# Attention on one core: value products in four 32-wide column tiles, denominators from pair sums

## The reference

```python
q, k = x @ wq_s, x @ wk_s                  # 8 heads of 16, over x normalised
attn = softmax(q @ k.T * 16 ** -0.5)       # per image and head, 1024 x 1024
v = x @ wv_r                               # 2 x 16 columns, shared by all heads
per_head = attn @ v                        # 1024 x (2 x 16), for each of 8 heads
sim = softmax over the 2 retrievals of (u . per_head) * 16 ** -0.5
out = sum over the 2 retrievals of sim * per_head
x = x + out @ w_out
```

## Time and profile before

| | us |
|---|---|
| median of 3 executions | 5733.49 |
| lowest, highest | 5732.6, 5741.53 |
| span of the profiled execution | 5736.7 |
| PE busy | 4699.7 (82%) |
| DVE busy | 3076.5 (54%) |
| ACT busy | 1975.9 (34%) |
| POOL busy | 633.7 (11%) |
| mean granted PE clock | 0.898 |

### The profile page before, as it was taken

One profiled execution on the slowest core, in us unless ns is written; L12 is line 12 of the kernel. 1 busy time (PEld: TensorE's weight loads), 2 busy tenths in 40 slices (PEclk: granted clock), 3 DMA queues, 4 the chain that ended last, 5 costly groups with the idle time before them and its releaser, 6 DMA issues. The chain is left out here.

```text
span 5736.7 us, 63937 instructions
## 1 busy us (share of the span) xinstructions
PE 4699.7 (82%) x19695; PEld 1764.3 (31%) x19695; DVE 3076.5 (54%) x5438; ACT 1975.9 (34%) x2773; POOL 633.7 (11%) x882
## 2 busy tenths in 40 slices
PE   4599999947699898888888888896699999855423
PEld 2233333315122222222222222223344444443212
DVE  4777777748666666556555555553300000357663
ACT  3211111127044444444444444455343434412200
POOL 1000000007101111111110110014100000201201
PEclk9799999979599999999999999998899999966655
DMA  1344444427411112222122222201000000112404
GB/s 63 79 103 91 92 99 92 95 82 262 66 21 19 19 21 27 27 27 27 23 27 27 27 27 27 27 5 50 29 0 0 0 0 0 54 64 80 122 0 128
DMA packets 173099, 290.74 MB, mean 51 GB/s; under 512 B 23207, under 2 KB 98989, under 8 KB 171453
## 3 DMA queue, kind: packets, MB, share of 16 engines
q1 hardware_dynamic: 144696, 252.65, 20.8%
q10 hardware_dynamic: 23808, 25.17, 1.2%
q0 software_dynamic: 4368, 10.07, 0.6%
HBM read 92.39 MB, written 67.63 MB: 28 GB/s over the span
## 5 line engine op out<-in xcount | busy, mean ns | idle before, releaser
L1474 DVE TENSOR_REDUCE at_mx<-at_side 128x1 f32<-128x512 f32 x2048 | 1336.6, 687 | 452.2 <-PE at_side L1387 445.8
L1543 ACT ACTIVATE at_P<-at_S 128x1024 f32<-128x1024 f32 x1024 | 997.1, 1024 | 1345.6 <-PE at_S L1412 1281.0
L1422 PE MATMUL at_pv<-at_P,at_rvb 128*64 128x512 f32 x4096 | 1113.1, 627 | 71.6 <-issue 54.1
L1387 PE MATMUL at_side<-at_ko,at_qo 96*128 96x512 bf16 x2048 | 757.7, 400 | 63.2 <-DMA at_ko<-qk 38.0
L1412 PE MATMUL at_S<-at_qo,at_ko 99*128 99x512 bf16 x2048 | 594.9, 381 | 22.6 <-DMA at_qo<-at_mrow 22.3
L1784 PE MATMUL ff_ph<-ffn_Y,ff_w 128*128 (+1 forms) x1024 | 525.5, 595 | 9.3 <-DMA ff_b<-in_b_dram 9.3
L1814 ACT ACTIVATE ff_hs<-ff_ph,ff_b 128x512 f32<-128x512 f32 x512 | 351.7, 687 | 525.3 <-PE ff_ph L1784 525.3
L1798 PE MATMUL ff_po<-ff_hs,ff_w2s 128*128 128x512 f32 x1024 | 523.2, 593 | 0.0
L616 PE MATMUL la_acc<-la_rep,la_wagg 128*32 128x512 f32 x4096 | 511.2, 606 | 1.1 <-DMA la_rep<-la_pad 1.1
L773 DVE SCALAR_TENSOR_TENSOR la_dwq<-la_pad,la_taps,la_dwq 128x1024 f32<-128x1024 f32 x384 | 491.7, 1280 | 7.2
L1833 DVE SCALAR_TENSOR_TENSOR X<-ff_po,ffn_b2w,X 128x512 f32 (+1 forms) x32 | 24.0, 751 | 823.8 <-PE ff_po L1798 823.8
(11 more groups left out here) (410 smaller groups left out, 4194.6 us busy)
## 6 DMA issues: line engine op xcount, KB each, us to landing
la_rep<-la_pad SPq DMA_DIRECT2D x512, 162.2 KB, 3.6
qk<-ap_part SPq DMA_DIRECT2D x32, 768.0 KB, 3.7
at_qo<-qk SPq DMA_DIRECT2D x96, 256.0 KB, 9.8
at_ko<-qk SPq DMA_DIRECT2D x96, 256.0 KB, 20.1
n_ln_xs<-X SPq DMA_DIRECT2D x96, 256.0 KB, 2.3
X<-in_x_dram SPq DMA_DIRECT2D x4, 2048.0 KB, 22.2
proj<-la_y POOLq DMA_DIRECT2D x32, 256.0 KB, 2.3
lan_y<-proj SPq DMA_DIRECT2D x8, 1024.0 KB, 5.0
```

Source lines behind the costliest of these rows:

```text
L1387: return pe.matmul(side[bank][:, :], qo[1 - u][0:KQ, s, i * C:(i + 1) * C], ko[1 - u][0:KQ, s, h * CH:(h + 1) * CH], start=True, stop=True)
L1422: last = pe.matmul(pv_acc[hp][64 * i:64 * i + 64, :], rvb[u][:, j, :], P[k % 2][:, 2 * hp + i, :], start=(j == 0), stop=(j == 7))
L1474: v.reduce_max(mx[:, n // 2, n % 2:n % 2 + 1], side[bank][:, :], AX.X).then_inc(side_saved, 1)
L1543: a.activation(P[k % 2][:, 2 * hp:2 * hp + 2, :], S[hp][:, :, :], ACT.Exp).then_inc(p_ready, 1)
```

## The change

Values of four heads go as four 32-wide column tiles into one accumulator `num`, with the 32 values alone as weights. For the denominators POOL adds the exponentials of two steps into one (`pair`), and PE multiplies the sum by 32 columns of ones, four heads side by side, into `den` (`totals`), after the values of each even step. `P` has four buffers in place of two; `exps` of an even step waits for the denominators that read its buffer. The order in a group becomes half first, then quad, so that half of the queries is finished for all heads in mid-slot, and retrieval, tokens, back and output run in two halves. Maxima run four a step in all 32 steps. The loads, maxima rows and `ub` are split in halves; values go through `u` in memory (columns 128 to 159 of it) in place of the tile `RV`.

```diff
-                        v.tensor_copy(us[w][:, 2 * h:2 * h + 2, :], puv[h][:, :, 0:C])
-                        v.tensor_copy(RV[:, bass.ds(4 * n + 2 * h, 2), :], puv[h][:, :, C:C + RVW]).then_inc(uv_saved, 1)
+                        v.tensor_copy(us[w][:, 2 * h:2 * h + 2, :], puv[h][:, :, :]).then_inc(uv_saved, 1)
...
-FIRST_MAX = 3
-LAST_MAX = STEPS - 4
-PER_STEP = -(-MAX_UNITS // (LAST_MAX + 1 - FIRST_MAX))
-EXP_AT, SUM_AT, OUT_AT, WOUT_AT = 13, 15, 19, 22
+QUAD = 4
+TOKENS_AT = (2, 18)
+BACK_AT = (5, 22)
+WOUT_AT = (6, 23)
+EXP_AT = (28, 12)
+SUM_AT = (30, 14)
+ROWS_AT = (17, 1)
...
-        P = [m.sb(f"P{u}", [C, 4, CH]) for u in range(2)]
+        P = [m.sb(f"P{u}", [C, QUAD, CH]) for u in range(4)]
...
+                    if not last and not is_first(b):
+                        sp.wait_ge(s_ready, 64 * b)
+                        load(b + 1, 1 - u, 1)
+                    if not last:
+                        wait_if(sp, pv_done, 32 * b)
+                        values_of(b + 1, 1 - u)
...
-                        sp.wait_ge(s_ready, 64 * b + 64)
-                        load(b + 2, u)
+                        sp.wait_ge(s_ready, 64 * b + 48)
+                        load(b + 2, u, 0)
...
+                def pair(b, i):
+                    g.wait_ge(p_ready, 64 * b + 4 * i + 4)
+                    g.wait_ge(pv_done, 32 * b + 2 * i + 1)
+                    a = 2 * i % 4
+                    g.tensor_tensor(P[a][:, :, :], P[a][:, :, :], P[a + 1][:, :, :], ALU.add).then_inc(pair_done, 1)
...
+                def slot(b, u, last):
+                    post = not is_first(b)
+                    for i in range(16):
+                        pair(b, i)
+                        if i == 0 and post:
+                            retrieve(b - 1, 0, 6, None)
+                        if 2 <= i <= 8 and post:
+                            retrieve(b - 1, 1, i - 2, side_at(b, ("tokens", 1, 3), last))
+                        if i >= 10:
+                            retrieve(b, 0, i - 10, side_at(b, ("tokens", 0, 3), last))
...
-                    for i in range(2):
-                        last = pe.matmul(pv_acc[hp][64 * i:64 * i + 64, :], rvb[u][:, j, :], P[k % 2][:, 2 * hp + i, :],
+                    pe.wait_ge(p_ready, 64 * b + 2 * k + 2)
+                    for i in range(QUAD):
+                        last = pe.matmul(num[32 * i:32 * i + 32, :], rvt[u][:, j, :], P[k % 4][:, i, :],
                                          start=(j == 0), stop=(j == 7))
...
+                def totals(b, k):
+                    j = (k - 2) % 8
+                    if j == 0:
+                        wait_if(pe, den_saved, 4 * b + k // 8)
+                    pe.wait_ge(pair_done, 16 * b + k // 2)
+                    for i in range(QUAD):
+                        last = pe.matmul(den[32 * i:32 * i + 32, :], K["ones"][:, 0:32], P[(k - 2) % 4][:, i, :],
+                                         start=(j == 0), stop=(j == 6))
+                    last.then_inc(den_done, 1)
...
+                        for part in range(3):
+                            for w in work[(part * len(work) + 1) // 3:((part + 1) * len(work) + 1) // 3]:
+                                fill(w, b, u, side_base(b) + at, bank_of(b, at)).then_inc(side_ready, 1)
+                                at += 1
+                            if part < 2:
+                                if k + 2 < STEPS:
+                                    scores(b, u, k + 2, part)
+                                elif not last:
+                                    scores(b + 1, 1 - u, k + 2 - STEPS, part)
+                        values(b, u, k)
+                        if k % 2 == 0 and not (first and k == 0):
+                            totals(b, k)
...
                 def exps(b, k):
+                    if k % 2 == 0:
+                        wait_if(a, den_done, 16 * b + k // 2 - 1)
                     for hp in range(2):
                         a.wait_ge(s_ready, 64 * b + 2 * k + hp + 1)
-                        wait_if(a, pv_done, 32 * b + k - 1)
-                        a.activation(P[k % 2][:, 2 * hp:2 * hp + 2, :], S[hp][:, :, :], ACT.Exp).then_inc(p_ready, 1)
+                        a.activation(P[k % 4][:, 2 * hp:2 * hp + 2, :], S[hp][:, :, :], ACT.Exp).then_inc(p_ready, 1)
...
+                        if k % 8 < 2 and (k >= 8 or not first):
+                            if k >= 8:
+                                save(b, k // 8 - 1, k % 8)
+                            else:
+                                save(b - 1, 3, k % 8)
```

More of the change, by code:

```diff
@@ L1210, with side_work @@
 MAX_UNITS = 128
-VW = 2 * RH * DH
-FIRST_MAX = 3
-LAST_MAX = STEPS - 4
-PER_STEP = -(-MAX_UNITS // (LAST_MAX + 1 - FIRST_MAX))
-EXP_AT, SUM_AT, OUT_AT, WOUT_AT = 13, 15, 19, 22
-def side_work(k, post, following):
+QUAD = 4
[5 more added lines that the diff above has]
+ROWS_AT = (17, 1)
+def side_work(k, first, last):
+    post = not first
     work = []
     if post:
[L1222 to L1231, removed]
+        if k == ROWS_AT[1]:
+            work.append(("rows", 1))
+        for n in range(4):
+            if k == TOKENS_AT[0] + n:
+                work.append(("tokens", 1, n))
+        for h in range(2):
+            if k == BACK_AT[h]:
+                work.append(("back", h))
+            if k == WOUT_AT[h]:
+                work.append(("wout", h))
+    for n in range(4):
+        if k == TOKENS_AT[1] + n:
+            work.append(("tokens", 0, n))
+    if not last:
+        if k == ROWS_AT[0]:
             work.append(("rows", 0))
+        work += [("max", n) for n in range(QUAD * k, QUAD * k + QUAD)]
     return work
+TAIL = ([("tokens", 1, n) for n in range(4)] + [("back", 0), ("wout", 0), ("back", 1), ("wout", 1)])
 def phase_attn(nc, K, D, X):
-    SIDE1 = MAX_UNITS + 1
-    SIDE2 = SIDE1 + 12
+    SIDE0 = MAX_UNITS + 2
+    SIDE1 = sum(len(side_work(k, True, False)) for k in range(STEPS))
+    SIDE2 = sum(len(side_work(k, False, False)) for k in range(STEPS))
+    SIDE3 = sum(len(side_work(k, False, True)) for k in range(STEPS))
+    assert SIDE2 % 2 == 0
     with Mem(nc, "at") as m:
@@ L1316, in slot @@
+                for z in range(2):
+                    load(0, 0, z)
+                values_of(0, 0)
+                for z in range(2):
+                    load(1, 1, z)
+                for z in range(2):
+                    rows(0, 0, z)
                 def slot(b, u, last):
-                    if not isinstance(b, int) or b:
-                        sp.wait_ge(side_ready, side_at(b, OUT_AT, ("back", 1), following=not last))
-                    sp.dma_start(ub[:, :, :], D["u"][:, bass.ds(8 * b, 8), :]).then_inc(u_in, 16)
+                    if not last and not is_first(b):
+                        sp.wait_ge(s_ready, 64 * b)
+                        load(b + 1, 1 - u, 1)
@@ L1375, in _ @@
+                over(g, B, slot)
+                retrieve(B - 1, 0, 6, None)
+                for part in range(7):
+                    retrieve(B - 1, 1, part, TAIL_BASE + 4)
             @block.tensor
@@ L1440, in slot @@
+                for z in range(2):
+                    pe.wait_ge(op_in[0][z], 192)
+                    for n in range(64 * z, 64 * z + 64):
+                        fill(("max", n), -1, 1, n + z, (n + z) % 2).then_inc(side_ready, 1)
+                    fill(("rows", z), z - 1, 1, 64 + 65 * z, (64 + 65 * z) % 2).then_inc(side_ready, 1)
                 def slot(b, u, last):
-                    post = not isinstance(b, int) or b > 0
+                    first = is_first(b)
                     at = 0
-                    pe.wait_ge(rv_ready, b + 1)
@@ L1571, in slot @@
                             exps(b + 1, 0)
-                        if k == EXP_AT and post:
-                            softmax2(b - 1)
-                        if k % 8 == 7:
-                            save(b, k // 8, post, last)
+                        if k == EXP_AT[1] and not first:
+                            softmax2(2 * b - 1)
+                        if k == EXP_AT[0]:
+                            softmax2(2 * b)
                 over(a, B, slot)
-                softmax2(B - 1)
+                for what in range(2):
+                    save(B - 1, 3, what)
+                softmax2(2 * B - 1)
 def phase_norm(nc, K, X, Y, tag, tokens=None):
@@ L2451, in build @@
         phase_linatt_norm(nc, K, D, X)
[L2452 to L2455 removed]
+        phase_attn_prep(nc, K, D, X)
+        phase_attn(nc, K, D, X)
         with Mem(nc, "ffn") as m:
```

359 lines of the change are left out of this document (191 added, 168 removed).

## The result

The changed kernel takes 5851.4 us (median of 4 runs, 5838.26 to 5856.9) against 5733.92 in the same comparison: 1.020 times as long, interval 1.0185 to 1.0214. I had forecast 5649, a gain. The profiled execution spans 5852.8.

A forecast was written before the change was run, and what follows sets the result against it. PE, 91% busy in attention, sets the pace now; after the change a ring of exponentials and denominators binds. Terms -193 + 60 - 19 - 9 + 56 + 8 + 13 = -84 gave 5649 us, range 5575 to 5755.

The forecast's parts named there:

- 14 x 142.9 + 60: Middle slots: 142.9 us each without load waits, against 138.9, plus 60 for waits and low clock at five loop jumps.
- First slot: Attention's first slot, without retrieval and with one copy pair less: 136.3 us against 127.8, +8.
- last: Attention's last slot, without maxima: 110.5 us against 98.0, +13.
- -19: Prologue: half the loads land 13 to 14 us sooner and the 4.91 wait for maxima rows goes; -19 us.
- tail: After attention, only the second half of the last image's retrieval is left, with POOL operations halved; -9 us.
- The ring: Attention steps: even-step exponentials wait for denominators, next scores for them; 8.06 us per two steps against 8.36.
- I take 0, by the nearest row that runs: DVE's splitting of maxima rows during POOL's pair sums, twice a slot: taken to cost 0, from a 0.284 us row.
- The upper end, +69: Row splitting waits for the rest of the pair sum: 2.3 us, 2 x 15 times, +69.
- The clock: Rival: PE's clock falls for a tenth of each slot, +150, giving 5800; chance 0.06.
- Loads: Half loads remove the waits at slot starts, -193 with clock; +60 returns at the loop jumps.
- POOL: POOL's pair sums in attention: 4.5 us each, 16 a slot, hidden with 6.8 of 9.2 us used.
- the second: Rival: DVE's row splitting waits for POOL's pair sums, +69, giving 5718; chance 0.25.

The follow-up runs named there:

- e1: The changed kernel with the remainder of the row maxima (`mleft`) in the free half of the PSUM side buffer instead of SBUF; 5739.2 us.
- after: The changed kernel itself, as measured and profiled, against the kernel before; 5851.4 us.
- e5: e1 with ACT's two copies of a group's sums behind the exponentials of the same step instead of ahead; 5567.6 us.
- e4: The kernel before with only its loads divided into halves of four heads, asked for at different steps; 5553.1 us.
- e7: e5 plus a separate buffer for POOL's pair sums and the second half-load asked for at step 2 of its own slot; 5359.9 us.
- e8: e4 with the second half-load asked for at step 2 of its own slot instead of step 30 of the one before; 5532.2 us.

## Why the prediction was wrong

The miss is 202 us: -84 forecast, +117.5 measured. In the profiled execution it is made of these, with about 1 left over:

- *Slots 1 to 14*, 159.85 on average, in sum 2238 against 14 x 142.9 + 60 = 2061: +177.
- First slot 142.3 against 136.3, last 121.1 against 110.5: +17.
- First value product at 1559.3 where -19 meant 1555, tail 27.5 us where -9 from 34 meant 25: +7.

The slots 1 to 14 of e1 (1701.4 to 3822.9) divide the 177. Undisturbed steps, 14 x 145.2 against 14 x 142.9, are 32 of it. The jumps and the slow steps of e1 are 89 where I had 60, which is 29. What after takes more than e1, 2238 against 2121, is the row splitting, 117.

Point by point:

- **The ring was right.** Pitches of 5.08 and 3.14 (5.00 in the peeled slots) against 4.91 and 3.15: 8.22 against 8.06. A slot from e1's undisturbed steps is 145.2, not 142.9: +32 over 14 slots. Blocks of 1.01, the 0.21 to the exponentials, and saves of 4.70 and 5.49, 2.0 more than plain steps (1.9 a group in the sum), came as read.
- **The step that failed: "I take 0, by the nearest row that runs".** The row was read at a time when POOL stood still, so it could not bear on an overlap. (The reduction at 2217.62, which the prediction puts beside POOL, doesn't overlap it either: POOL's last operation there ended at 2216.78. Others, as that at 2208.74, did, at their usual pace, but they read PSUM.) The upper end, +69, was too small as well. It took the rest of the pair sum, 2.3, at each place; measured, the two steps at a place in slot 13 take 14.8 instead of 9.4. Of these 5.4, 2.6 is the cast, 1.0 the next operation of POOL (not in the bound at all), and 1.8 is left over, which I put down to the half clock behind the pause. 28 x 5.4 = 152 in these slots; the net price is 117 there and 112 in the medians, since e1 has slow steps at some of the same places. The rule that the prediction takes from the Trainium skill (SBUF — State Buffer, "Who interferes with whom") holds here: the operation with two SBUF inputs went from 0.28 to 1.27 us. The same section of the Trainium skill says that a cast too can contend for the shared ports. The cast, with one SBUF input, was blocked for longer here (2.88 for 0.21), and I had left it out.
- **The clock was mis-sized.** I gave its fall a chance of 0.06 and looked for it in a busy share. It came behind single pauses, of 1.2 to 1.4 us at the saves and of 1.74 at the row splitting. By e5 it costs some 54 in e1 alone (the estimate above); in the sum it stood at 0 outside the jumps.
- **Loads.** Right in direction: e4 alone gives -183, prologue included, against -193 + 60 - 19 = -152. At the jumps ACT's wait fell from 62.8 to 41.7 after (28.7 in e4), and a step there takes 11.6 to 12.9 in place of 4.63, which is 37 in all, with some clock behind it; I had kept 60 for both.
- **POOL** as forecast: 4.52, and 3.1 us of waits.

The forecast range, 5575 to 5755, was left by 96 us. Of the rivals, the second was the mechanism, and its price was too low. Even with it removed the kernel is no faster than before (e1), since ring, copies and clock eat the 183 that the loads give. What the rest of the change, the value tiles above all, is worth shows once the three are gone: e7 against e8, 5359.9 against 5532.2, 3.1%, with second halves of the loads asked for at the same step. (The copies keep their place in e8, but its steps behind a group are 4.18 long like the plain ones, so they cost little there.) e7 is the fastest kernel here, 6.6% under before.

## What to carry to other kernels

Where a change puts GpSimd to work, list each VectorE instruction that reads SBUF with two operands or casts from it, and price it at the rest of GpSimd's operation, plus the next in its queue, plus the clock that PE loses behind the pause. A row read while GpSimd stands still says nothing about it. Where engine time is saved and the order makes a ring (a buffer freed by the last thing in a step), follow the ring first, and take copies and in-place sums off it: here each was worth 168 to 179 us. Take each part of a bundle alone: the divided loads gave 183 us, and the bundle lost 117.

## What the hardware showed that I had not expected

- A cast of 32x128 from SBUF, 0.21 us alone, took up to 3.92 us beside a GpSimd sum, and the operation behind it lost a second time, to GpSimd's next operation (1.27 for 0.28). From PSUM both take 0.28 under the same sum.
- Four 32-wide tiles run eight passes in the 1.01 us of two 64-wide ones; a second block with other weights starts 0.88 behind the first (2209.64 to 2210.52), and the next full-array matmul 1.86 (2211.50).
- PE pauses of 1.1 to 1.7 us were followed at times by 4 to 8 us at a granted clock of 0.56 to 0.78. The plain steps' pauses of 0.90 were not, in e1 and e5.
- Instructions behind a loop jump came up to 2.0, 7.0 or 13.0 us late with nothing, half a load (1.5 MB) or a whole one (3 MB) in flight.
